# A feed-forward block with fp32 weights and one fp32 product per tile, in place of bf16 weights and two bf16 products

## The chip, the cores and the metric

The kernel runs on one Trainium2 chip, on all 8 NeuronCores at once. Each core computes half of the tokens of one of four sequences and needs nothing from the others. The metric is the device time of one execution in microseconds, which is that of the slowest core.

## The reference

```python
def reference(x, wq, wk, wv, wo, w_gate_up, w_proj):      # x: (4, 2048, 2048) fp32
    x = x + layernorm(attention(layernorm(x), wq, wk, wv, wo))   # 16 heads of 128, causal
    x = x + layernorm(ffn(layernorm(x), w_gate_up, w_proj))
    return x

def ffn(x, w_gate_up, w_proj):                # 16384 x 2048 and 2048 x 8192, fp32
    gu = einsum('bsd,hd->bsh', x, ternary_quant(w_gate_up))
    gate, up = split(gu, 2)
    h = silu(gate) * up                       # 8192 wide
    return einsum('bsh,dh->bsd', rms_norm(h), ternary_quant(w_proj))

def ternary_quant(w_fp32, g=64):              # all of it in bf16
    w = w_fp32.astype(bfloat16)
    scale = clip(mean(abs(groups of 64 of w)), 1e-8)
    w_hat = clip(round(w / scale), -1, 1) * scale
    return w + (w_hat - w)
```

## The kernel before

Everything on the chip is held transposed: features on the 128 partitions, tokens in the free dimension. A core has 1024 tokens of its own and the 2048 tokens of its sequence for keys and values. A small planner (`Prog.emit`) writes one list of instructions per engine, in program order, with semaphore waits; nothing is reordered afterwards. A DMA that an engine issues waits on that engine's queue, so a late wait on the sync queue (SP) holds back every later load.

The stages follow each other:

- **`_attn1`** loops over 4 token blocks of 512. For each it normalises the block and then makes 16 output tiles each of k, v and q. A tile is 16 fp32 matmuls (128x128 weights, 512 columns for k and v, 256 for q) whose weights come in one slab of 1 MB, loaded into one of two halves of `AR_W` (lines 378 and 421). The v tiles are transposed on TensorE, copied to `ptb` (line 471) and stored to `v_scr`, with waits on earlier stores.
- **`_quant_gen`** runs between the tiles of `_attn1`, one step for each of the 192 tiles. A step makes the ternary weights of a 128x2048 piece. GpSimd issues its load (fp32 in DRAM, bf16 in SBUF, line 293), does the last two operations (lines 278 and 282) into the bf16 tile `QLND`, and issues the store to `wgu_hat` or `wp_hat` (line 286). There are two `QLND` buffers; a step waits for the store of the step two before.
- **`_attn2`** is the attention itself, head by head. **`_attn3`** is the output projection: 2 token blocks, each of 16 slabs of 16 fp32 matmuls with 512 columns (line 664), slab loads two ahead, and then the layer norm and the residual.
- **`_ffn`** loops over 4 blocks `fb` of 256 tokens. A block loads x1 (line 709) and normalises it into `AR_D` (`_ln_block`, its last DVE operations at lines 368 and 371). DVE then splits the 16 pieces of the result into a bf16 high part `LN2H` (line 721) and a bf16 low part `LN2L` (line 723).

In the **gate-up loop** of `_ffn` there are 64 steps `c`. A step needs two weight slabs of 512 KB, one for gate (line 733) and one for up (line 738), in one of two pairs of buffers; the load of a pair waits for the matmuls that last used it. The pair for c=1 waits for all that was issued before it, c=0 included. A step is 64 matmuls of 256 columns: 16 pieces, gate and up (lines 748 and 755), high and low part. Then ACT computes silu (line 761), DVE multiplies (line 764) and splits the product into `HH` and `HL` (lines 768 and 771), ACT squares it (line 774), and TensorE adds the square into a sum (line 778). This last matmul stands ahead of the next step's matmuls in TensorE's order.

In the **projection loop** there are 16 output tiles of 64 pieces, in 4 slabs each. Every slab load (line 812) waits for all matmuls emitted so far:

```python
wsl = [("sP", P_.cnt["sP"] if (sw or dm or ss) else 0)]
```

So a slab's load starts when the matmuls of the slab before have ended. A slab is 32 matmuls of 256 columns (line 827). A last layer norm, the residual and the store to `out` close the block.

Of the kernel before, what the change touches and what calls it, by code (L numbers as in the profile page):

```python
# [106 lines left out]
def _alloc(nc):  # L107
# [13 lines left out]
    for nm, shape, dt_ in (("wgu_hat", [D, GU], BF16), ("wp_hat", [HF, D], BF16),  # L121
                           ("k_scr", [D, S], F32), ("v_scr", [S, D], F32),
                           ("q_scr", [D, TOK], F32), ("x1_scr", [D, TOK], F32)):
        if nm in _DBG_OUTS:
            DR[nm] = nc.dram_tensor(nm, shape, dt_, kind="ExternalOutput").ap()
        else:
            DR[nm] = nc.dram_tensor(nm, shape, dt_).ap()
# [37 lines left out]
    T["AR_WB"] = at("AR_WB", [128, 8192], BF16, 180224)  # L165

# [530 lines left out]
def _ffn(P_, T, DR):  # L697
# [3 lines left out]
    l2h = lambda k: T["LN2H"].ap()[:, k * 256:(k + 1) * 256]  # L701
    l2l = lambda k: T["LN2L"].ap()[:, k * 256:(k + 1) * 256]
    hh = lambda c: T["HH"].ap()[:, c * 256:(c + 1) * 256]
    hl = lambda c: T["HL"].ap()[:, c * 256:(c + 1) * 256]
    wb = lambda q: T["AR_WB"].ap()[:, q * 2048:(q + 1) * 2048]

    x1_ok = P_.snap("dC") + P_.snap("dQ")
    for fb in range(4):
# [9 lines left out]
        sp = None  # L718
        for k in range(KC):
            ws = [("sV", ln2_done), ("sP", P_.cnt["sP"])] if k == 0 else []  # L720
            P_.emit("dve", lambda e, k=k: e.tensor_copy(out=l2h(k), in_=lnD(k)),
                    waits=ws, inc="sV", tag=f"fsh{fb}.{k}")
            sp = P_.emit("dve", lambda e, k=k: e.tensor_tensor(  # L723
                out=l2l(k), in0=lnD(k), in1=l2h(k), op=ALU.subtract),
                inc="sV", tag=f"fsl{fb}.{k}")
        slabs = {}
        hsq_mm = None
        for c in range(64):
            r = c % 2
# [13 lines left out]
            mmu = None
            for k in range(KC):
                ws = [sl_g, sl_u, ("sV", sp)] if k == 0 else []
                for p, rhs_f in ((0, l2h), (1, l2l)):
                    P_.emit("pe", lambda e, gbank=gbank, r=r, k=k, rhs_f=rhs_f, p=p:
                            e.matmul(gbank, wb(2 * r)[:, k * 128:(k + 1) * 128],  # L748
                                     rhs_f(k), start=(k == 0 and p == 0),
                                     stop=(k == KC - 1 and p == 1)),  # L750
                            waits=ws if p == 0 else [], inc="sP",
                            tag=f"fg{fb}.{c}.{k}.{p}")
                    ws = []
                    mmu = P_.emit("pe", lambda e, ubank=ubank, r=r, k=k, rhs_f=rhs_f,
                                  p=p: e.matmul(  # L755
                                      ubank, wb(2 * r + 1)[:, k * 128:(k + 1) * 128],
                                      rhs_f(k), start=(k == 0 and p == 0),
                                      stop=(k == KC - 1 and p == 1)),
                                  inc="sP", tag=f"fu{fb}.{c}.{k}.{p}")
            slabs[r] = mmu  # L760
            sv = P_.emit("act", lambda e, gbank=gbank: e.activation(  # L761
                out=T["tmp"].ap()[:, 0:256], in_=gbank, func=AF.Silu),
                waits=[("sP", mmu)], inc="sA", tag=f"fsilu{fb}.{c}")
            ht = P_.emit("dve", lambda e, ubank=ubank: e.tensor_tensor(  # L764
                out=T["tmp"].ap()[:, 256:512], in0=T["tmp"].ap()[:, 0:256],
                in1=ubank, op=ALU.mult),
                waits=[("sA", sv)], inc="sV", tag=f"fht{fb}.{c}")
            P_.emit("dve", lambda e, c=c: e.tensor_copy(
                out=hh(c), in_=T["tmp"].ap()[:, 256:512]), inc="sV",
                tag=f"fhh{fb}.{c}")  # L770
            hv = P_.emit("dve", lambda e, c=c: e.tensor_tensor(
                out=hl(c), in0=T["tmp"].ap()[:, 256:512], in1=hh(c),
                op=ALU.subtract), inc="sV", tag=f"fhl{fb}.{c}")
            hq = P_.emit("act", lambda e: e.activation(
                out=T["LNXB"].ap()[:, 0:256], in_=T["tmp"].ap()[:, 256:512],
                func=AF.Square),
                waits=[("sV", ht)], inc="sA", tag=f"fhsq{fb}.{c}")
# [23 lines left out]
        for sw in range(2):  # L801
            for dm in range(8):
# [3 lines left out]
                for ss in range(4):  # L806
                    half = ss % 2
                    wsl = [("sP", P_.cnt["sP"] if (sw or dm or ss) else 0)]
                    if dc == 0 and ss == 0:
# [3 lines left out]
                                     out=wb(half).rearrange(  # L813
# [6 lines left out]
                    for kk in range(16):  # L820
# [4 lines left out]
                        for p, h_f in ((0, hh), (1, hl)):  # L825
                            mm = P_.emit("pe", lambda e, bank=bank, half=half,
                                         kk=kk, hk=hk, h_f=h_f, p=p: e.matmul(  # L827
                                             bank, wb(half)[:, kk * 128:
                                                            (kk + 1) * 128],
                                             h_f(hk), start=(hk == 0 and p == 0),  # L830
                                             stop=(hk == 63 and p == 1)),
                                         waits=ws if p == 0 else [], inc="sP",
                                         tag=f"fp{fb}.{dc}.{hk}.{p}")
                            ws = []
# [123 lines left out]
```

How the kernel before makes its waits and increments, by code:

```python
        def rnd(eng_obj, recs, own_sem=None):  # L71
            last_own = 0
            for waits, fn, inc, post, tag in recs:
                if own_sem is not None and last_own > 0 and fn is not None:
                    eng_obj.wait_ge(sems[own_sem], last_own)
                for (sem, v) in waits:
                    if v > 0:
                        eng_obj.wait_ge(sems[sem], v)
                if fn is not None:
                    ins = fn(eng_obj)
                    if inc is not None:
                        ins.then_inc(sems[inc], 16 if inc.startswith("d") else 1)
                if inc == own_sem and post is not None:
                    last_own = post
```

## Time and profile before

| | us |
|---|---|
| median of 2 runs | 16716.96 (16678.73 to 16755.19) |
| the profiled execution, its own time | 16731.51 |
| its span on the slowest core (core 1) | 16729.6 |
| spans of the 8 cores | 16537.4 to 16729.6 |
| attention, first to last instruction before the feed-forward block, core 1 | 0 to 10983 |
| feed-forward block, core 1 | 10983 to 16730 |

The spans are those of one execution under the profiler. A "record" below is one entry of the trace for one instruction. A matmul record's duration includes the drain of the array, so successive records overlap; the distance between their starts is what one costs in a stream. "PEclk" is the clock that the throttle granted to TensorE as a share of full speed. The mean over the whole run lies between 0.678 and 0.689 on the 8 cores.

### The profile page before, as it was taken

How to read it: one execution, taken by the hardware profiler on the slowest of the kernel's cores; microseconds unless marked ns; L12 is line 12 of the kernel's file. 1: busy time of each engine (PE TensorE's matmuls, PEld its weight loads, DVE VectorE, ACT ScalarE, POOL GpSimd, SP SyncE). 2: the span in 40 equal slices, each digit the busy share in tenths (PEclk: the TensorE clock that was granted, in tenths of full speed). 3: DMA queues.
4: the chain of work that ended last, by engine and by line, in shares of the span. 5: the costliest groups of instructions: out<-in, count | busy, mean ns of one | idle time of the engine just before them, and what ended most of it. 6: DMA issues, size and time to landing. Idle time of an engine off the chain costs nothing.

```text
span 16729.6 us, 137588 instructions; the slowest of 8 cores (16537.4 to 16729.6 us)
## 1 busy us (share of the span) xinstructions
PE 10050.8 (60%) x39456; PEld 5798.5 (35%) x39456; DVE 4080.1 (24%) x8274; ACT 1926.1 (12%) x2699; POOL 1768.1 (11%) x772
## 2 busy tenths in 40 slices
PE   6655866776676544444444546757548655754864
PEld 2222323223222322222222223336326434533643
DVE  3334434434443422222222221121011001001100
ACT  2122212222222200000000000000000000000000
POOL 2233323223332300000000000000000000000000
PEclk7666666666667655555555557879769768966976
DMA  3223323232332300000000001234224224422422
GB/s 83 68 75 83 85 68 89 80 80 77 86 82 72 93 7 13 7 13 7 13 7 13 7 13 30 71 92 102 52 54 115 66 46 96 92 52 63 113 59 48
DMA packets 2253436, 992.82 MB, mean 59 GB/s; under 512 B 1605317, under 2 KB 2178886, under 8 KB 2250566
## 3 DMA queue, kind: packets, MB, share of 16 engines
q1 hardware_dynamic: 2137542, 732.31, 17.3%
q0 software_dynamic: 55296, 201.35, 5.4%
q10 hardware_dynamic: 59904, 50.36, 0.9%
q8 instruction: 380, 6.23, 0.2%
q14 instruction: 314, 2.57, 0.1%
HBM read 925.17 MB, written 159.38 MB: 65 GB/s over the span
## 4 chain that ended last, share of the span: by engine, by line
PE 54%; DVE 15%; DMA 12%; issue 8%; ACT 5%; POOL 3%; DVEq 1%; ACTq 0%; SPq 0%; POOLq 0%
PE pbG L421 14%; PE pbH L623 7%; DMA AR_WB<-wp_hat 6%; PE pbG L748 6%; PE pbH L755 5%; PE pbG L610 3%; DMA v_scr<-ptb 3%; DVE ptb L617 3%; PE pbG L664 3%; PE pbE L531 3%; PE pbF L827 2%; PE pbE L827 2%; PE pbH L827 2%; PE pbG L827 2%; POOL QLND L282 2%
## 5 line engine op out<-in xcount | busy, mean ns | idle before, releaser
L421 PE MATMUL pbG<-AR_C,AR_W 128*128 128x512 f32 x4096 | 2369.5, 751 | 102.3 <-DVE AR_C L371 102.3
L623 PE MATMUL pbH<-ptb,AR_B 128*128 128x128 f32 x2944 | 1128.7, 487 | 1047.1 <-DVE ptb L617 1047.1
L421 PEld LDWEIGHTS pbG<-AR_C,AR_W 128*128 128x128 f32 x4096 | 970.8, 241 | 1437.2 <-issue 1437.2
L610 PE MATMUL pbG<-ident_t,AR_B 128*128 128x128 f32 x1472 | 656.2, 446 | 976.2 <-DVE AR_B L597 973.5
L748 PE MATMUL pbG<-LN2H,AR_WB 128*128 128x256 bf16 x4096 | 1127.5, 275 | 180.9 <-DVE LN2L L723 128.4
L623 PEld LDWEIGHTS pbH<-ptb,AR_B 128*128 128x128 f32 x2944 | 738.2, 312 | 1436.4 <-issue 1436.4
L278 POOL TENSOR_TENSOR QSG<-QT,QW 128x2048 bf16<-128x2048 bf16 x192 | 776.6, 4045 | 3871.0 <-DVE QT L273 3871.0
L755 PE MATMUL pbH<-LN2H,AR_WB 128*128 128x256 bf16 x4096 | 1128.3, 275 | 0.0
L748 PE MATMUL pbG<-LN2L,AR_WB 128*128 128x256 bf16 x4096 | 1128.0, 275 | 0.0
L755 PE MATMUL pbH<-LN2L,AR_WB 128*128 128x256 bf16 x4096 | 1127.8, 275 | 0.0
L617 DVE COPY ptb<-pbG 128x128 f32<-128x128 f32 x1472 | 428.8, 291 | 2209.4 <-PE pbG L610 2209.4
L230 DVE TENSOR_SCALAR QSCL<-pbE 2x512 bf16<-2x512 f32 x768 | 523.0, 681 | 1448.4 <-PE pbE L222 1301.2
L282 POOL TENSOR_TENSOR QLND<-QW,QSG 128x2048 bf16<-128x2048 bf16 x192 | 777.1, 4047 | 39.7 <-POOL QSG L278 39.4
L222 PE MATMUL pbE<-QABS,b_t 128*2 128x512 bf16 x768 | 265.7, 551 | 854.2 <-ACT QABS L208 713.4
L610 PEld LDWEIGHTS pbG<-ident_t,AR_B 128*128 128x128 f32 x1472 | 267.5, 182 | 1343.0 <-issue 1334.9
L421 PE MATMUL pbH<-AR_C,AR_W 128*128 128x256 f32 x2048 | 658.0, 499 | 0.0
L764 DVE TENSOR_TENSOR tmp<-tmp,pbH 128x256 f32<-128x256 f32 x256 | 107.8, 421 | 2071.1 <-ACT tmp L761 2071.1
L531 PE MATMUL pbE<-AR_B 128*128 128x512 f32 x480 | 443.1, 1074 | 261.7 <-DMA AR_B<-q_scr 203.6
L421 PEld LDWEIGHTS pbH<-AR_C,AR_W 128*128 128x128 f32 x2048 | 522.2, 259 | 134.5 <-issue 28.2
L263 DVE TENSOR_TENSOR QT<-QABS,QBB 128x512 bf16<-128x512 bf16 x768 | 535.2, 697 | 97.4 <-DVE QBB L257 37.7
L273 DVE TENSOR_TENSOR QT<-QT,QBB 128x512 bf16<-128x512 bf16 x768 | 531.5, 692 | 83.2 <-DVE QT L268 4.1
L827 PE MATMUL pbE<-HH,AR_WB 128*128 128x256 bf16 x1024 | 358.8, 367 | 284.9 <-DMA AR_WB<-wp_hat 284.9
(123 smaller groups left out, 11406.2 us busy)
## 6 DMA issues: line engine op xcount, KB each, us to landing
AR_WB<-wgu_hat SPq DMA_DIRECT2D x512, 512.0 KB, 6.3
AR_WB<-wp_hat SPq DMA_DIRECT2D x256, 512.0 KB, 4.1
QW<-wguT POOLq DMA_DIRECT2D x128, 512.0 KB, 8.6
AR_W<-wkT SPq DMA_DIRECT2D x64, 1024.0 KB, 9.2
wgu_hat<-QLND POOLq DMA_DIRECT2D x128, 512.0 KB, 5.9
AR_W<-wvT SPq DMA_DIRECT2D x64, 1024.0 KB, 5.7
AR_W<-wqT SPq DMA_DIRECT2D x64, 1024.0 KB, 6.0
QW<-wpT POOLq DMA_DIRECT2D x64, 512.0 KB, 7.9
```

The lines of the kernel that those rows point to most:

```text
L263: t_tok[(i, q)] = P_.emit("dve", lambda e, q=q: e.tensor_tensor(out=tt[:, q * 512:(q + 1) * 512], in0=absw[:, q * 512:(q + 1) * 512], in1= ...
L273: tsg_tok[(i, q)] = P_.emit("dve", lambda e, q=q: e.tensor_tensor(out=tt[:, q * 512:(q + 1) * 512], in0=tt[:, q * 512:(q + 1) * 512], in1= ...
L278: d_tok[i] = P_.emit("gp", lambda e: e.tensor_tensor(out=sg, in0=tt, in1=w, op=ALU.subtract), waits=[("sV", tsg_tok[(i, 3)])], inc="sG", t ...
L282: wf = P_.emit("gp", lambda e: e.tensor_tensor(out=laund, in0=w, in1=sg, op=ALU.add), waits=ws, inc="sG", tag=f"q_wf{i}")
L421: e.matmul(bank, T["AR_W"].ap()[:, half * 2048 + k * 128: half * 2048 + (k + 1) * 128], rhs, start=(k == 0), stop=(k == KC - 1)),
L531: mm = P_.emit("pe", lambda e, t_=t_, c_=c_, kb=kb, qt=qt: e.matmul(t_[:, c_:c_ + 512], qh[:, qt * 128:(qt + 1) * 128], kh[:, kb * 512:(kb ...
L610: tr = P_.emit("pe", lambda e, trb=trb, kc=kc: e.transpose(trb, prob[:, kc * 128:(kc + 1) * 128], T["ident"][:]), waits=ws, inc="sP", tag= ...
L617: te = P_.emit("dve", lambda e, trb=trb, pcol=pcol: e.tensor_copy(out=T["ptb"].ap()[:, pcol:pcol + 128], in_=trb), waits=tew, inc="sV", ta ...
L623: e.matmul(abank, vT[:, kc * 128:(kc + 1) * 128], T["ptb"].ap()[:, pcol:pcol + 128], start=(kc == 0), stop=(kc == W // 128 - 1)),
L748: e.matmul(gbank, wb(2 * r)[:, k * 128:(k + 1) * 128], rhs_f(k), start=(k == 0 and p == 0), stop=(k == KC - 1 and p == 1)),
L755: p=p: e.matmul(ubank, wb(2 * r + 1)[:, k * 128:(k + 1) * 128], rhs_f(k), start=(k == 0 and p == 0), stop=(k == KC - 1 and p == 1)),
L827: kk=kk, hk=hk, h_f=h_f, p=p: e.matmul(bank, wb(half)[:, kk * 128: (kk + 1) * 128], h_f(hk), start=(hk == 0 and p == 0), stop=(hk == 63 an ...
```

## The change

The quantised weights are kept in DRAM as fp32 in place of bf16, and the feed-forward block multiplies fp32 by fp32. What does that is this:

- `wgu_hat` and `wp_hat` are F32 tensors. GpSimd's store of a quantised piece now converts from bf16 to fp32 on its way and writes 1 MB, not 512 KB.
- The weight slabs in SBUF are four fp32 buffers of 1 MB (`FSLAB`) at another address, where `LN2H` and `LN2L` were.
- The two DVE operations per piece that made `LN2H` and `LN2L` are gone, and so are the two that made `HH` and `HL`. DVE writes the fp32 product directly into `hf32(c)`.
- Each pair of matmuls (high and low part against the same bf16 weights) becomes one fp32 matmul: 32 in place of 64 for a gate-up step, 16 in place of 32 for a projection slab.
- The first gate-up loads of a block wait also for DVE's and ACT's last emitted instruction, that is, for the end of the layer norm. Before, they waited for TensorE's alone.

```diff
-    for nm, shape, dt_ in (("wgu_hat", [D, GU], BF16), ("wp_hat", [HF, D], BF16),
+    for nm, shape, dt_ in (("wgu_hat", [D, GU], F32), ("wp_hat", [HF, D], F32),
...
+    T["FSLAB"] = at("FSLAB", [128, 8192], F32, 65536)
...
+    hf32 = lambda c: T["AR_A"].ap()[:, c * 256:(c + 1) * 256]
+    fsl = lambda q: T["FSLAB"].ap()[:, q * 2048:(q + 1) * 2048]
...
-        sp = None
-        for k in range(KC):
-            ws = [("sV", ln2_done), ("sP", P_.cnt["sP"])] if k == 0 else []
-            P_.emit("dve", lambda e, k=k: e.tensor_copy(out=l2h(k), in_=lnD(k)),
-                    waits=ws, inc="sV", tag=f"fsh{fb}.{k}")
-            sp = P_.emit("dve", lambda e, k=k: e.tensor_tensor(
-                out=l2l(k), in0=lnD(k), in1=l2h(k), op=ALU.subtract),
-                inc="sV", tag=f"fsl{fb}.{k}")
...
-            wsl = [("sP", slabs[r])] if r in slabs else                 [("sP", P_.cnt["sP"])] + list(x1_ok)
+            wsl = [("sP", slabs[r])] if r in slabs else                 [("sP", P_.cnt["sP"]), ("sV", P_.cnt["sV"]),
+                 ("sA", P_.cnt["sA"])] + list(x1_ok)
...
-                ws = [sl_g, sl_u, ("sV", sp)] if k == 0 else []
-                for p, rhs_f in ((0, l2h), (1, l2l)):
...
+                ws = [sl_g, sl_u, ("sV", ln2_done)] if k == 0 else []
+                P_.emit("pe", lambda e, gbank=gbank, r=r, k=k:
+                        e.matmul(gbank, fsl(2 * r)[:, k * 128:(k + 1) * 128],
+                                 lnD(k), start=(k == 0), stop=(k == KC - 1)),
+                        waits=ws, inc="sP", tag=f"fg{fb}.{c}.{k}")
+                mmu = P_.emit("pe", lambda e, ubank=ubank, r=r, k=k: e.matmul(
+                    ubank, fsl(2 * r + 1)[:, k * 128:(k + 1) * 128],
+                    lnD(k), start=(k == 0), stop=(k == KC - 1)),
+                    inc="sP", tag=f"fu{fb}.{c}.{k}")
...
-            P_.emit("dve", lambda e, c=c: e.tensor_copy(
-                out=hh(c), in_=T["tmp"].ap()[:, 256:512]), inc="sV",
-                tag=f"fhh{fb}.{c}")
-            hv = P_.emit("dve", lambda e, c=c: e.tensor_tensor(
-                out=hl(c), in0=T["tmp"].ap()[:, 256:512], in1=hh(c),
-                op=ALU.subtract), inc="sV", tag=f"fhl{fb}.{c}")
...
-                        for p, h_f in ((0, hh), (1, hl)):
...
+                        mm = P_.emit("pe", lambda e, bank=bank, half=half,
+                                     kk=kk, hk=hk: e.matmul(
+                                         bank, fsl(half)[:, kk * 128:
+                                                         (kk + 1) * 128],
+                                         hf32(hk), start=(hk == 0),
+                                         stop=(hk == 63)),
+                                     waits=ws, inc="sP",
+                                     tag=f"fp{fb}.{dc}.{hk}")
```

## Rows read from the trace of the kernel before

**Rows 1.** Spans and mean granted TensorE clock of two cores.

```profile
core 1: 16729.6 us, clock 0.686
core 2: 16673.3 us, clock 0.679
```

**Rows 2.** Windows, core 1: length, busy PE, PEld, DVE, ACT, POOL (records), PEclk, DMA share, GB/s.

```profile
11061.00:11647.00 586.00, 469.63 (x4091) 396.19 (x4092) 70.68 (x186) 49.66 (x124) 0.00 (x0) 0.99 0.49 114
11665.00:12340.00 675.00, 366.91 (x2052) 258.15 (x2052) 19.52 (x48) 7.46 (x18) 0.00 (x0) 0.71 0.22 49
```

**Rows 3.** SP's issues, core 1: gate slab loads of two steps, and the x1 loads.

```profile
11096.21 0.36 SPq L733 DMA_DIRECT2D AR_WB<-wgu_hat  x1
...
11105.36 0.36 SPq L733 DMA_DIRECT2D AR_WB<-wgu_hat  x1
...
L709 SPq DMA_DIRECT2D AR_D<-x_scr x4: 367/370/370, 10982.8 to 15289.7; - x4
```

**Rows 4.** Timeline of PE, core 1, gate-up (start us, us): two records, 15 apart.

```profile
11099.82 0.27 PE L748 MATMUL pbG<-LN2H,AR_WB 128*128 128x256 bf16 x1
...
11101.46 0.27 PE L755 MATMUL pbH<-LN2L,AR_WB 128*128 128x256 bf16 x1
```

**Rows 5.** Projection, core 1: 63 loads on SP; then PE's total wait for them.

```profile
11665.04 633.89 SPq L812 DMA_DIRECT2D AR_WB<-wp_hat  x63
...
  DMA AR_WB<-wp_hat: 1142.6, 256
```

**Rows 6.** fp32 matmuls, core 1: chain row of attn3, q burst, windows in that burst.

```profile
10648.61 221.91 PE pbG L664 x512
...
1124.67 9.45 PE L421 MATMUL pbH<-AR_C,AR_W 128*128 128x256 f32 x32
...
1124.70:1134.50 9.80, 9.41 (x33) 7.60 (x32) 7.90 (x15) 1.60 (x4) 0.00 (x0) 0.77 0.00 0
...
1130.00:1133.00 3.00, 3.00 (x16) 2.64 (x15) 2.51 (x5) 0.00 (x0) 0.00 (x0) 1.00 0.00 0
```

**Rows 7.** DMA issues: count, KB each, median us from issue to landing.

```profile
AR_WB<-wgu_hat SPq DMA_DIRECT2D x512, 512.0 KB, 6.3
AR_WB<-wp_hat SPq DMA_DIRECT2D x256, 512.0 KB, 4.1
AR_W<-wkT SPq DMA_DIRECT2D x64, 1024.0 KB, 9.2
...
AR_W<-woT SPq DMA_DIRECT2D x32, 1024.0 KB, 5.5
```

**Rows 8.** Block start, core 1: first and last of 32 split operations; PE's slab waits.

```profile
11032.80 0.29 DVE L721 CAST LN2H<-AR_D 128x256 bf16<-128x256 f32 x1 [0.24 <-DVE AR_D L371]
...
11047.44 0.42 DVE L723 TENSOR_TENSOR LN2L<-AR_D,LN2H 128x256 bf16<-128x256 f32 x1
...
PE pbG L748 <- DMA AR_WB<-wgu_hat: 31.9, 4, 8.8
```

**Rows 9.** Core 2: windows of attn3 and of gate-up 1 and 4; loads as rows 3.

```profile
9844.00:10100.00 256.00, 255.53 (x485) 108.46 (x486) 0.00 (x0) 8.96 (x15) 0.00 (x0) 0.81 0.21 61
10760.00:11300.00 540.00, 453.09 (x3254) 353.00 (x3255) 57.41 (x151) 40.00 (x100) 0.00 (x0) 0.80 0.42 98
...
15340.00:15900.00 560.00, 458.65 (x3766) 377.24 (x3765) 66.12 (x174) 46.40 (x116) 0.00 (x0) 0.93 0.47 109
...
11101.96 0.36 SPq L733 DMA_DIRECT2D AR_WB<-wgu_hat  x1
...
11144.41 0.36 SPq L733 DMA_DIRECT2D AR_WB<-wgu_hat  x1
...
L709 SPq DMA_DIRECT2D AR_D<-x_scr x4: 366/370/370, 10617.6 to 15213.1; - x4
```

**Rows 10.** Core 1: GpSimd's wait (us, times, longest); chain of v phase 1 by line.

```profile
POOL QSG L278 <- DVE QT L273: 3871.0, 192, 152.3
...
by line: PE pbG L421 50.6%; DMA v_scr<-ptb 23.0%; ACT QABS L208 5.0%; issue 4.7%; PE pbF L245 4.0%; PE pbE L222 3.4%; DVE ptb L471 2.0%; DVE QSCL L230 1.8%; PE pbH L460 1.5%; ACT stg L448 1.5%; PE pbE L245 1.1%; ACTq L478 0.5%; ACTq L78 0.3
```

More of the change, by code:

```diff
@@ L700, in _ffn @@
     lnY = lambda k: T["AR_D"].ap()[:, 4096 + k * 256: 4096 + (k + 1) * 256]
[L701 to L705, printed above, removed]
+    hf32 = lambda c: T["AR_A"].ap()[:, c * 256:(c + 1) * 256]
+    fsl = lambda q: T["FSLAB"].ap()[:, q * 2048:(q + 1) * 2048]
     x1_ok = P_.snap("dC") + P_.snap("dQ")
@@ L731, in _ffn @@
             ubank = (pbH[:, 0:256], pbH[:, 512:768])[r]
-            wsl = [("sP", slabs[r])] if r in slabs else                 [("sP", P_.cnt["sP"])] + list(x1_ok)
+            wsl = [("sP", slabs[r])] if r in slabs else                 [("sP", P_.cnt["sP"]), ("sV", P_.cnt["sV"]),
+                 ("sA", P_.cnt["sA"])] + list(x1_ok)
             sl_g = P_.emit("sync", lambda e, c=c, r=r: e.dma_start(
-                out=wb(2 * r).rearrange("p (kk t) -> p kk t", kk=16),
+                out=fsl(2 * r).rearrange("p (kk t) -> p kk t", kk=16),
                 in_=DR["wgu_hat"].rearrange("(kk p) m -> p kk m", p=128)[
@@ L738, in _ffn @@
             sl_u = P_.emit("sync", lambda e, c=c, r=r: e.dma_start(
-                out=wb(2 * r + 1).rearrange("p (kk t) -> p kk t", kk=16),
+                out=fsl(2 * r + 1).rearrange("p (kk t) -> p kk t", kk=16),
                 in_=DR["wgu_hat"].rearrange("(kk p) m -> p kk m", p=128)[
@@ L744, in _ffn @@
             for k in range(KC):
-                ws = [sl_g, sl_u, ("sV", sp)] if k == 0 else []
-                for p, rhs_f in ((0, l2h), (1, l2l)):
[L747 to L759, printed above, removed]
+                ws = [sl_g, sl_u, ("sV", ln2_done)] if k == 0 else []
[7 more added lines that the diff above has]
+                    inc="sP", tag=f"fu{fb}.{c}.{k}")
             slabs[r] = mmu
@@ L763, in _ffn @@
                 waits=[("sP", mmu)], inc="sA", tag=f"fsilu{fb}.{c}")
-            ht = P_.emit("dve", lambda e, ubank=ubank: e.tensor_tensor(
-                out=T["tmp"].ap()[:, 256:512], in0=T["tmp"].ap()[:, 0:256],
+            hprev = [("sP", hsq_mm)] if c >= 1 else []
+            ht = P_.emit("dve", lambda e, ubank=ubank, c=c: e.tensor_tensor(
+                out=hf32(c), in0=T["tmp"].ap()[:, 0:256],
                 in1=ubank, op=ALU.mult),
                 waits=[("sA", sv)], inc="sV", tag=f"fht{fb}.{c}")
-            P_.emit("dve", lambda e, c=c: e.tensor_copy(
-                out=hh(c), in_=T["tmp"].ap()[:, 256:512]), inc="sV",
-                tag=f"fhh{fb}.{c}")
-            hv = P_.emit("dve", lambda e, c=c: e.tensor_tensor(
-                out=hl(c), in0=T["tmp"].ap()[:, 256:512], in1=hh(c),
-                op=ALU.subtract), inc="sV", tag=f"fhl{fb}.{c}")
[L774 to L777, printed above, removed]
+            hq = P_.emit("act", lambda e, c=c: e.activation(
+                out=T["LNXB"].ap()[:, 0:256], in_=hf32(c), func=AF.Square),
+                waits=[("sV", ht)] + hprev, inc="sA", tag=f"fhsq{fb}.{c}")
             hsq_mm = P_.emit("pe", lambda e, c=c: e.matmul(
@@ L812, in _ffn @@
                                  e.dma_start(
-                                     out=wb(half).rearrange(
+                                     out=fsl(half).rearrange(
                                          "p (kk t) -> p kk t", kk=16),
@@ L824, in _ffn @@
                             ws.append(("sV", yv[7]))
-                        for p, h_f in ((0, hh), (1, hl)):
[L826 to L834, printed above, removed]
+                        mm = P_.emit("pe", lambda e, bank=bank, half=half,
[6 more added lines that the diff above has]
+                                     tag=f"fp{fb}.{dc}.{hk}")
                 yv[dm] = P_.emit("dve", lambda e, bank=bank, dc=dc: e.tensor_tensor(
```

## The prediction

> **What bounds the kernel now.** I read the spans and granted clocks first. The slowest core is core 1 with 16729.6 us, and core 2 is 56 us behind it [rows 1]; the execution itself took 16731.5 us, 14.5 us over the median of 16717, so the sum below is made against 16731 and holds for the median within 0.1%. Then the windows of the feed-forward block on core 1. Gate-up has 64 steps in 586 us with TensorE busy 80% of it at a granted clock of 0.99 [rows 2]. One step takes 11105.36 - 11096.21 = 9.15 us [rows 3]. Fifteen record starts lie 1.64 us apart, so a 256-column bf16 matmul costs 0.1093 us [rows 4], 64 of them 7.00 us, and the other 2.15 us are the tail silu, multiply, square, sum matmul, during which TensorE stands still. The slab loads aren't in it: they land 6.3 us after issue [rows 7] and are issued a whole step ahead. Gate-up is thus bound by TensorE's stream plus a fixed tail.
>
> The projection is bound by TensorE and the loads in turn. 63 loads take 633.89 us, so one slab takes (633.89 - 0.36) / 62 = 10.22 us; TensorE waits 1142.6 / 256 = 4.46 us for each, and a burst of 32 matmuls takes the rest, 5.7 us [rows 5]. At full clock it would take 3.5 us. The mean clock there is 0.71 [rows 2]: every burst starts at the lower level (1.2 GHz) after its wait and rises to 2.4 GHz some 4 us in. A block lasts (15289.7 - 10982.8) / 3 = 1435.6 us [rows 3], of which 586 + 654 are these two loops.
>
> **The fp32 matmul.** A token block of the output projection has 16 x 16 = 256 fp32 matmuls of 512 columns and shows 512 records in 221.91 us [rows 6]. So an fp32 matmul is two records. Taking off some 2 us for the slow start, a record costs 0.4295 us at full clock, and half of it, 0.2147 us, with 256 columns. The q tiles have just that shape: 32 records in 9.45 us with a clock of 0.77 [rows 6]. From 0.77, 46% of the window or 4.5 us were at half clock; 32 x 0.2147 + 4.5 / 2 = 9.1 us, and 9.45 less the last record's drain is the same. The weight loads (PEld, 2.64 us in a full-clock window of 3 us) stay below the matmuls and are hidden [rows 6]. The change replaces two bf16 matmuls (0.219 us) by two fp32 records (0.429 us): TensorE's time for this work doubles, less nothing.
>
> **Gate-up.** 64 bf16 matmuls become 64 fp32 records: 64 x (0.2147 - 0.1093) = 6.75 us more per step, 9.15 -> 15.9 us, times 256 steps: **+1728 us**. The tail stays: the two split operations removed from DVE there start after the multiply, and what waits for the multiply (ACT's square) does not wait for them; they are worth nothing. The loads double to 2 MB per 15.9 us, 132 GB/s against 114 now [rows 2]. A pair issued a step ahead has 15.9 us to land. I take it as hidden; a pair would have to take over two and a half times today's 6.3 us to show.
>
> **Projection.** The burst: 32 fp32 records. With 4.2 to 4.5 us at half clock, 32 x 0.2147 + 2.2 = 9.1 us against 5.7, +3.4. The wait: the slab grows from 512 KB to 1 MB and its load isn't covered by anything. The nearest row is the slab of wo, same size, rows and stride, on an otherwise quiet machine: 5.5 us to landing against 4.1 [rows 7], +1.4 us. The bounds are 0 (a landing set by the number of pieces, which stays) and +5.1 (the wk slabs, 9.2 us, beside the quantiser's traffic [rows 7]). I take 1.4, as nothing else loads then. Sum +4.8 us, 256 slabs: **+1230 us** (low 870, high 2180).
>
> **Block starts.** The 32 split operations last from 11032.80 to 11047.86, 15.1 us with nothing beside them [rows 8]. They go. In their place the first pair of slabs, whose load now waits for the end of the layer norm, is exposed: the pair for c=1 is exposed today at up to 8.8 us for 1 MB, a mean of 8.0 [rows 8]; for 2 MB I take 10 us. So -5 us for c=0 and +2 for c=1: **-3 us** per block, -12 in all (between -30 and +20).
>
> **The quantiser.** The store of 1 MB goes out on GpSimd's queue, where only the next load is queued behind it. GpSimd idles 3871 us over 192 steps, 20 us each [rows 10], and a buffer has two steps until it is needed, so the store itself is hidden; without that cover it would be 192 times some 3 us. But it shares the DMA engines with the small v stores, which are 23% of the chain in the v phase [rows 10], some 500 us over the four. The trace has no store of that kind; the bound above is the 1.4 us that 512 KB more cost a slab [rows 7], on both store waits of 64 tiles, 180 us; below, nothing. I take **+80 us**.
>
> Sum on core 1: 1728 + 1230 - 12 + 80 = +3026, **19757 us**, if its clock stays as it is.
>
> **The clock.** Core 1 is not the core to look at. On core 2 the granted clock stands at 0.81 through the output projection, where 485 records take 256 us: 0.528 us each, which is 0.4295 / 0.81. It stands at 0.80 through gate-up and is back at 0.93 only in block 4 [rows 9]. Core 2 starts the feed-forward block 365 us before core 1, loses most of this through the lower clock and ends 56 us ahead [rows 1, 3, 9]. Its gate-up step takes (11144.41 - 11101.96) / 4 = 10.61 us, 0.132 us per matmul. After the change an fp32 record costs it 0.528 / 2 = 0.264: 64 x (0.264 - 0.132) = 8.4 us per step, 540 per block. In the projection the burst at full speed is some 22 records, 0.05 us longer each: 4.8 + 1.1 - 0.2 = 5.7 us per slab, 365 per block. So a block under this clock costs +902, one without (1728 + 1230 - 12) / 4 = +737. With core 2 held in three blocks of four as today: 16673 + 3 x 902 + 737 + 80 = 20196. **I forecast 20200 us**, set by core 2 or one like it.
>
> The Trainium skill (TensorE: Matmul & The Clock Gate, Part 1, the peak-current limiter) says that dense matmuls on three cores of a die take that die to 13/16 of the clock for as long as the load lasts. The 0.81 of rows 9 agrees in size; core 1's 0.99 in gate-up, while all cores work [rows 2], doesn't agree. By the page no core would see full clock, which is the third rival.
>
> **Rivals.**
> - *Core 2 is not released.* The longer, denser stream keeps 0.81 in block 4 too: + (902 - 737) and the 76 us by which that block was shorter than the mean of the first three (1532): 20440.
> - *The clock holds no one back in the feed-forward block.* Then core 1 sets the end: 19757. Against it: fp32 is the denser stream, 86% of a step instead of 77%.
> - *The limit takes core 1 in the feed-forward block as well.* Its four blocks would then cost 4 x (1532 + 902) from 10983 + 80: 20800.
> - *The loads show.* Projection slabs land as those of wk do: +3.7 x 256 = 950, 21150 with core 2. A quiet wo-like machine speaks against it.
> - *Not slower.* An fp32 matmul would have to be one record of bf16 cost, as if weights holding bf16 values took a short way. The 512 and 32 records speak against it. It would be 12288 records of 0.109 fewer, -1343, and + 360 for loads - 12 + 80: 15816. It decides where the mean fp32 record falls under 0.105 us, half of what is measured.
>
> **Chances.** Forecast 0.38; core 2 not released 0.20; no hold 0.15; core 1 held too 0.15; loads show 0.07; not slower 0.02; others 0.03. About 2% is what a measurement can tell from no change; all cases but one lie far above 17050, so slower 0.98, within 2% 0.01, faster 0.01. The range takes in the first four cases and leaves room for the projection's low bound: 19650 to 20850.
>
> **What would show it.** Right: fp32 records of 0.21 to 0.22 us spacing at clock 1.0, steps of 15.9 us and of 19.0 on a held core; projection waits of 5.9 us and bursts of 9.1; splits gone and 10 us of slab wait in their place; a v phase longer by 1 to 2 us per tile. Wrong: waits for slabs between gate-up steps, a landing far from 5.5, a burst that starts at full clock, or another pattern of 0.81 over the cores.

## The result, and the profile after

| | before | after |
|---|---|---|
| median, us | 16784.61 (10 runs, 16645.83 to 17259.89) | 20381.9 (11 runs, 20118.74 to 20885.64) |
| ratio of after to before | | 1.2114, 95% interval 1.2028 to 1.22 |
| profiled span of the slowest core, us | 16729.6 (core 1) | 20333.6 (core 0) |

The change made the kernel 21% slower. The forecast was 20200 us (19650 to 20850), slower with a chance of 0.98. The runs of before behind the ratio are more than the two known at the time of the forecast; their median is 68 us higher. Some executions of either kernel are some per cent longer, because the cores of one die are granted less clock in them; the medians and ranges include these, the ratios leave them out.

First the page of the slowest core after the change: the costliest matmul groups (count | busy us, mean ns of one | idle before, releaser) and the weight loads (count, KB each, us to landing).

```profile
L738 PE MATMUL pbG<-AR_D,FSLAB 128*128 128x256 f32 x8192 | 2791.9, 426 | 177.0 <-DMA FSLAB<-wgu_hat 159.4
L741 PE MATMUL pbH<-AR_D,FSLAB 128*128 128x256 f32 x8192 | 2766.9, 423 | 0.0
```

```profile
FSLAB<-wgu_hat SPq DMA_DIRECT2D x512, 1024.0 KB, 10.0
FSLAB<-wp_hat SPq DMA_DIRECT2D x256, 1024.0 KB, 5.5
```

The number of records is that of before: 16384 in gate-up, two for each fp32 matmul where there were two bf16 matmuls. The wp slab of 1 MB lands in 5.5 us, which is what the wo slab of the same size took [rows 7].

The gate-up loop and the clock, in windows (length, busy PE, PEld, DVE, ACT, POOL, PEclk, DMA share, GB/s). The first two rows are gate-up of blocks 1 and 3 on core 0, the next two the projection of blocks 2 and 3 there, the last two gate-up of blocks 1 and 3 on core 2; they answer to [rows 2, 9].

```profile
11000.00:12100.00 1100.00, 1003.67 (x3560) 816.16 (x3560) 22.75 (x54) 43.16 (x108) 0.00 (x0) 0.77 0.39 105
16000.00:17000.00 1000.00, 880.39 (x3735) 737.99 (x3734) 26.59 (x60) 47.26 (x116) 0.00 (x0) 0.94 0.45 119
...
14700.00:15600.00 900.00, 571.29 (x1787) 455.08 (x1785) 5.95 (x14) 0.00 (x0) 0.00 (x0) 0.70 0.22 65
17300.00:17800.00 500.00, 312.99 (x1052) 252.91 (x1053) 3.40 (x8) 0.00 (x0) 0.00 (x0) 0.78 0.23 67
...
10800.00:11700.00 900.00, 806.12 (x3434) 676.99 (x3434) 21.91 (x52) 41.56 (x104) 0.00 (x0) 0.94 0.43 124
...
15600.00:16500.00 900.00, 821.04 (x2915) 667.77 (x2916) 18.53 (x44) 35.52 (x89) 0.00 (x0) 0.77 0.42 105
```

There are two levels in gate-up. One is 0.77 to 0.79, a core held at 0.81 with short stretches at half clock. The other is 0.94, where the kernel before had 0.99 [rows 2]. Core 0 is held in blocks 1 and 2 and free in 3 and 4, core 2 the other way round. Each core is thus held in two blocks of four, and the eight cores end within 158 us of one another.

Now the part that was not foreseen. SP's gate loads on core 0 in block 3, one per step (start us, us), and TensorE over the start of one of those steps:

```profile
16213.68 0.36 SPq L724 DMA_DIRECT2D FSLAB<-wgu_hat  x1
...
16229.79 0.36 SPq L724 DMA_DIRECT2D FSLAB<-wgu_hat  x1
...
16247.59 0.36 SPq L724 DMA_DIRECT2D FSLAB<-wgu_hat  x1
```

```profile
16231.37 0.27 PE L757 MATMUL pbE<-LNXB,ones_t 128*1 128x256 bf16 x1 [1.71 <-ACT LNXB L754]
16231.72 0.67 PE L738 MATMUL pbG<-AR_D,FSLAB 128*128 128x256 f32 x2
16232.23 0.74 PE L741 MATMUL pbH<-AR_D,FSLAB 128*128 128x256 f32 x2
16232.76 1.06 PE L738 MATMUL pbG<-AR_D,FSLAB 128*128 128x256 f32 x2
16233.62 1.06 PE L741 MATMUL pbH<-AR_D,FSLAB 128*128 128x256 f32 x2
...
16236.07 0.59 PE L738 MATMUL pbG<-AR_D,FSLAB 128*128 128x256 f32 x2
16236.51 0.59 PE L741 MATMUL pbH<-AR_D,FSLAB 128*128 128x256 f32 x2
```

Steps take 16.11 or 17.80 us. Before the sum matmul of each of these steps TensorE stands still for 1.71 us; below, this standstill is the gap. In the kernel before it was 1.66 us:

```profile
11088.59 0.27 PE L778 MATMUL pbE<-LNXB,ones_t 128*1 128x256 bf16 x1 [1.66 <-ACT LNXB L774]
```

In a step of 17.80 us, pairs of fp32 records start 0.43 us apart at full clock, but soon after the gap they start 0.85 us apart for about 3.5 us, at the lower of the two levels (1.2 GHz). That costs some 1.7 us. A core is called free here where its clock is not held at 0.81. On a free core the mean step is 17.05 us, because the clock falls in 56% of the steps; on held cores it is 19.5 to 20.0 us.

The projection in the chain of waits on core 0, block 3 (start us, us): load, burst, load, burst.

```profile
17264.17 5.54 DMA FSLAB<-wp_hat
17269.84 9.02 PE pbE L805 x32
17278.98 5.49 DMA FSLAB<-wp_hat
17284.60 10.16 PE pbE L805 x32
```

The total wait of TensorE for these slabs, which answers to the 1142.6 us of [rows 5], is

```profile
  DMA FSLAB<-wp_hat: 1495.9, 256
```

that is 5.84 us each against 4.46. A slab takes 15.3 to 16.2 us against 10.2.

### The profile page after: what moved, and what is told of

It is laid out like the page before. It is cut to its first block, busy times and chain, and to the rows that moved or that the text cites. A ratio compares the mean times of both kernels' runs of the same rounds, so it can differ in the third digit from the quotient of the medians.

```text
span 20333.6 us, 136568 instructions; the slowest of 8 cores (20176.0 to 20333.6 us)
## 1 busy us (share of the span) xinstructions
PE 13332.2 (66%) x39456; PEld 8635.6 (42%) x39456; DVE 3851.1 (19%) x7634; ACT 1925.1 (9%) x2699; POOL 1768.4 (9%) x772
## 4 chain that ended last, share of the span: by engine, by line
PE 61%; DMA 12%; DVE 11%; issue 7%; ACT 5%; POOL 3%; DVEq 1%; ACTq 0%; SPq 0%; POOLq 0%
PE pbG L422 11%; PE pbG L738 10%; PE pbH L741 10%; DMA FSLAB<-wp_hat 7%; PE pbH L624 6%; PE pbH L805 3%; PE pbF L805 3%; PE pbG L805 3%; PE pbE L805 3%; PE pbG L611 3%; PE pbG L665 3%; DVE ptb L618 2%; PE pbE L532 2%; DMA v_scr<-ptb 2%; POOL QLND L283 1%
## 5 line engine op out<-in xcount | busy, mean ns | idle before, releaser
L738 PE MATMUL pbG<-AR_D,FSLAB 128*128 128x256 f32 x8192 | 2791.9, 426 | 177.0 <-DMA FSLAB<-wgu_hat 159.4
L741 PE MATMUL pbH<-AR_D,FSLAB 128*128 128x256 f32 x8192 | 2766.9, 423 | 0.0
L738 PEld LDWEIGHTS pbG<-AR_D,FSLAB 128*128 128x128 f32 x8192 | 1742.5, 215 | 516.2 <-issue 230.2
L741 PEld LDWEIGHTS pbH<-AR_D,FSLAB 128*128 128x128 f32 x8192 | 1765.4, 216 | 303.5
L805 PE MATMUL pbH<-AR_A,FSLAB 128*128 128x256 f32 x2048 | 629.9, 482 | 373.6 <-DMA FSLAB<-wp_hat 373.6
L805 PE MATMUL pbG<-AR_A,FSLAB 128*128 128x256 f32 x2048 | 626.4, 480 | 377.6 <-DMA FSLAB<-wp_hat 377.6
L805 PE MATMUL pbF<-AR_A,FSLAB 128*128 128x256 f32 x2048 | 627.7, 481 | 371.5 <-DMA FSLAB<-wp_hat 371.5
L805 PE MATMUL pbE<-AR_A,FSLAB 128*128 128x256 f32 x2048 | 618.0, 475 | 373.2 <-DMA FSLAB<-wp_hat 373.2
L805 PEld LDWEIGHTS pbH<-AR_A,FSLAB 128*128 128x128 f32 x2048 | 505.8, 251 | 497.9 <-issue 398.9
L805 PEld LDWEIGHTS pbG<-AR_A,FSLAB 128*128 128x128 f32 x2048 | 503.1, 249 | 502.1 <-issue 403.9
```

The source lines that it names most:

```text
L738: e.matmul(gbank, fsl(2 * r)[:, k * 128:(k + 1) * 128], lnD(k), start=(k == 0), stop=(k == KC - 1)),
L741: mmu = P_.emit("pe", lambda e, ubank=ubank, r=r, k=k: e.matmul(ubank, fsl(2 * r + 1)[:, k * 128:(k + 1) * 128], lnD(k), start=(k == 0), s ...
L805: kk=kk, hk=hk: e.matmul(bank, fsl(half)[:, kk * 128: (kk + 1) * 128], hf32(hk), start=(hk == 0), stop=(hk == 63)),
```

## The experiments

The theory: each step and each slab costs more for the reasons of the sum, and gate-up has an extra loss, the fall of the clock at the 1.7 us gap. Rivals: the extra loss comes from the projection half; it comes from the longer step and not from fp32; or fp32 drops the clock with or without a gap. One more was not thought of beforehand, and the traces speak to it: the change altered the gap itself, which is 0.05 us longer than before. Each run is compared with runs of the kernel before on the same chip; these had medians of 16640 us for `e1` to `e4`, 16643 us for `e5`, `e7`, `e8` and `e9`, and 16617 us (one run) for `e6` and `e12`.

### One half at a time

`e1` has fp32 in gate-up alone, `e2` in the projection alone.

```diff
# e1, from the changed kernel (with the projection loop of before)
-    for nm, shape, dt_ in (("wgu_hat", [D, GU], F32), ("wp_hat", [HF, D], F32),
+    for nm, shape, dt_ in (("wgu_hat", [D, GU], F32), ("wp_hat", [HF, D], BF16),
...
# e2, from the kernel before (with the projection loop of the change)
-    for nm, shape, dt_ in (("wgu_hat", [D, GU], BF16), ("wp_hat", [HF, D], BF16),
+    for nm, shape, dt_ in (("wgu_hat", [D, GU], BF16), ("wp_hat", [HF, D], F32),
...
```

> Only the gate-up half of the change: w_gate_up in fp32 and fp32 matmuls there, the projection as before (bf16 weights, high and low part). The recorded sum had gate-up at +6.75 us a step, 256 steps, and -12 us at block starts: about +1720, some 18500 us. The trace of the changed kernel shows steps of 17.05 us where the clock is not held and 19.5 to 20.05 where it is, against 9.2 and 10.7 before. If that is the gate-up loop's own doing, this kernel gains 7.85 x 256 = 2010 us with no core held, and some 2300 with two blocks of four held: 18800 to 19150 us. If the longer steps come from what the projection half does to the clock, it stays at 18500 and the step at 15.9 us.

> Only the projection half of the change: w_proj in fp32 and fp32 matmuls there, gate-up as before. The recorded sum had +4.8 us a slab, 256 slabs: +1230, some 18000 us, as +3.4 for the burst and +1.4 for the wait. The changed kernel's trace has a wait of 5.84 us (+1.38) and blocks of 966 to 1020 us for 64 slabs against 643 to 646: +5.0 to +5.8 us a slab, 1290 to 1490 us. Expected 18000 to 18250. e1 and e2 should add up to the whole change within some 150 us; if they do not, the two halves act on each other through the clock.

Measured: `e1` 18763.18 us (4 runs, 18575.73 to 18855.13), +2123 on its before (ratio 1.1238, interval 1.1106 to 1.1369); `e2` 18336.39 us (4 runs, 18155.44 to 18513.24), +1697. Gate-up windows of blocks 1 and 4 in `e1` on core 0, and one of its sum matmuls:

```profile
11200.00:12200.00 1000.00, 897.04 (x3813) 752.29 (x3812) 67.25 (x177) 47.20 (x118) 0.00 (x0) 0.94 0.43 122
...
17000.00:18000.00 1000.00, 897.16 (x3798) 752.07 (x3797) 67.25 (x177) 47.20 (x118) 0.00 (x0) 0.94 0.51 123
```

```profile
11311.79 0.27 PE L766 MATMUL pbE<-LNXB,ones_t 128*1 128x256 bf16 x1 [1.66 <-ACT LNXB L762]
```

With bf16 in the projection the gate-up clock is 0.94 all the same, and the steps take 17.05 us in all four blocks of this core. So the loss is the gate-up loop's own. The gap is 1.66 us here, as in the kernel before, and the clock falls after 59% of the gaps of this core; before, on free cores, it fell after 3 to 5%. `e1` ends just below what was expected, because in its profiled execution the slowest core is not held in this part at all.

`e2` ends above its range. Its projection takes 966 to 1012 us a block, about as expected, but its bf16 gate-up steps take 10.2 to 10.8 us in the mean of a block, against 9.2 to 9.3 on core 1 before. This is not the hold at 0.81. Core 0 is free in block 3, and its clock is 0.90 there, with bf16 records alone; the timeline is that of a gap in block 1, where it is free too:

```profile
14600.00:15150.00 550.00, 451.94 (x3486) 363.38 (x3484) 22.73 (x54) 43.16 (x108) 0.00 (x0) 0.90 0.44 104
```

```profile
11016.36 0.27 PE L775 MATMUL pbE<-LNXB,ones_t 128*1 128x256 bf16 x1 [1.71 <-ACT LNXB L772]
...
11017.47 0.27 PE L758 MATMUL pbH<-LN2L,AR_WB 128*128 128x256 bf16 x1
11017.58 0.27 PE L751 MATMUL pbG<-LN2H,AR_WB 128*128 128x256 bf16 x1
...
11018.07 0.42 PE L758 MATMUL pbH<-LN2L,AR_WB 128*128 128x256 bf16 x1
11018.28 0.42 PE L751 MATMUL pbG<-LN2H,AR_WB 128*128 128x256 bf16 x1
```

From 11017.86 to 11021.06 the bf16 records start 0.21 us apart in place of 0.11: the lower level. The clock falls after 56 to 61% of the gaps in this bf16 stream, and steps take 9.22 or 10.87 us. TensorE's own work in this loop is that of the kernel before. What differs around it is the gap, 1.71 us against 1.66, and that DVE no longer makes its two split operations beside it; `e2` does not separate these two. The 0.05 us come from the tail: the product goes to `AR_A` and the square reads it there, and the square starts 0.57 us after the multiply has started, where it was 0.51. All kernels with the product in `AR_A` and the gap left in (`e2`, `e4`, `e7`, the change) show 1.71, those with it in `tmp` (before, `e1`, `e3`, `e12`) 1.66.

The two halves add up to 3820 us, the whole change to 3597. The falls are one likely reason: they come in `e1` and in `e2`, some 240 us a core in each, and only once in the whole. Single executions scatter by about as much, so the difference proves nothing by itself.

### Is it the fp32 stream or the longer step?

```diff
# e3: the kernel before, each step's sums made twice
-            for k in range(KC):
+            for k in list(range(KC)) * 2:
# e4: the changed kernel, half of the pieces
-            for k in range(KC):
+            for k in range(KC // 2):
...
-                    lnD(k), start=(k == 0), stop=(k == KC - 1))
+                    lnD(k), start=(k == 0), stop=(k == KC // 2 - 1))
```

> The kernel before, with every gate-up step's 64 bf16 matmuls issued twice (the second set starts the sums anew, so the result stays): a bf16 stream of 14.0 us and then the same tail of 2.15 us with 1.7 us of standstill. In the changed kernel the clock falls to the lower level after about two of three such tails, before it almost never did. Theory kind: the fall hangs on fp32 records. Then this kernel keeps a granted clock of 0.98 to 1.0 in gate-up and a step is 16.15 us. Theory length: the fall hangs on the longer step around the same tail. Then the clock is 0.94, steps are 16.1 and 17.8 us mixed, mean 17.0.

> The changed kernel with only the first 8 of the 16 pieces multiplied in gate-up (half of the sum over features is left out): 32 fp32 records, a stream of 6.9 us and the same tail, so a step as long as the one before the change. Theory kind: the clock still falls after many tails; each fall costs some 1.7 to 2 us, the mean clock in gate-up is 0.85 to 0.92 and the mean step 9.9 to 10.7 us. Theory length: the clock stays at 0.98 or more as before and the step is 9.0 us. The loads of 2 MB a step now have 9 us to land, against 10.0 to landing in the changed kernel, so waits for slabs may show between steps; the clock at the start of a step that did not wait for a slab tells the theories apart.

Measured: `e3` 18592.22 us (2 runs, 18472.74 and 18711.69), `e4` 19088.82 us (1 run; it leaves out half of each sum). `e3` on core 0 in block 2: a window; two gate loads on SP; and the sum matmul after the second on TensorE.

```profile
12700.00:13600.00 900.00, 802.72 (x7163) 697.14 (x7160) 63.11 (x167) 44.47 (x112) 0.00 (x0) 1.00 0.28 65
```

```profile
13001.64 0.36 SPq L733 DMA_DIRECT2D AR_WB<-wgu_hat  x1
...
13017.77 0.36 SPq L733 DMA_DIRECT2D AR_WB<-wgu_hat  x1
```

```profile
13019.29 0.27 PE L778 MATMUL pbE<-LNXB,ones_t 128*1 128x256 bf16 x1 [1.66 <-ACT LNXB L774]
```

A step of 16.13 us with the gap of 1.66 us, and the clock stays at 1.00. On free cores it falls after 2 to 3% of these gaps. `e1` is its counterpart, with the same gap and nearly the same step (16.05 us without a fall), and there it falls after 59%. So on a free core, at this gap, the length of the step does not bring the fall and the change to fp32 does. On a held core the length counts too. In block 1 on core 2 of `e3` the bf16 clock falls below the 0.81 after 66% of gaps of 1.66 us; in the kernel before, with its short steps, it did so after 19% on the same core. The window:

```profile
10900.00:11800.00 900.00, 820.51 (x5877) 651.09 (x5876) 52.48 (x138) 36.84 (x92) 0.00 (x0) 0.78 0.24 55
```

`e4` in block 3 on core 2 is the other side, an fp32 step as short as that of bf16, here one in which no slab was waited for:

```profile
15021.55 0.27 PE L757 MATMUL pbE<-LNXB,ones_t 128*1 128x256 bf16 x1 [1.71 <-ACT LNXB L754]
15021.90 0.67 PE L738 MATMUL pbG<-AR_D,FSLAB 128*128 128x256 f32 x2
...
15023.15 1.06 PE L738 MATMUL pbG<-AR_D,FSLAB 128*128 128x256 f32 x2
15024.01 1.06 PE L741 MATMUL pbH<-AR_D,FSLAB 128*128 128x256 f32 x2
...
15026.25 0.59 PE L738 MATMUL pbG<-AR_D,FSLAB 128*128 128x256 f32 x2
```

The clock falls, in a step of 10.9 us. Its gap is 1.71 us, and `e2` shows the same with bf16 at such a gap, so `e4` shows only that a fall needs no long step; by itself it says nothing of fp32. The kind of matmul, what happens at the gap and, on a held core, the length all move the share of gaps with a fall. Which property of the stream lies behind them is open. The price of `e4` is not that of falls alone: its loads land 12.5 us after issue on core 2 (up to 14.4 on others), later than a step is long, so many steps wait for a slab, 4.4 us in the step before this one. Its mean steps are 12.4 to 14.3 us, well above the 9.9 to 10.7 expected. It also marks where the hidden gate-up loads stop being hidden.

### Taking the gap away

```diff
             slabs[r] = mmu
+            if pend is not None:
+                hsq_mm = pend()
...
-            hsq_mm = P_.emit("pe", lambda e, c=c: e.matmul(
-                pbE[0:1, 0:256], T["ones1"][:], T["LNXB"].ap()[:, 0:256],
+            pend = lambda c=c, r=r, hq=hq, fb=fb: P_.emit("pe", lambda e: e.matmul(
+                pbE[0:1, 0:256], T["ones1"][:],
+                T["LNXB"].ap()[:, r * 512:r * 512 + 256],
...
+        hsq_mm = pend()
```

> The changed kernel with the sum matmul of step c issued behind the matmuls of step c+1 (squares in two buffers), so TensorE does not stand still between gate-up steps. Theory gap: the clock falls in the changed kernel because an fp32 stream is interrupted for 1.7 us. Then without the gap the granted clock in gate-up is 1.0 where a core is not held, a step is 64 x 0.2147 + 0.1 = 13.85 us against 17.05, and the whole is some 800 us shorter, 19550 us. Theory kind alone: fp32 records drop the clock whatever stands between them. Then the clock stays at 0.94 and a step is 14.7 us, 19800 us. If the denser stream makes the 0.81 hold catch both groups of cores at once, steps are 17.0 us in more than two of four blocks and the time stays above 19900.

Measured: 19332.04 us (4 runs, 19267.78 to 19396.23), some 200 us less than expected. `pend()` issues the sum matmul of the step before. Core 0: a window in gate-up of block 1, and the gate loads of two steps on SP.

```profile
11200.00:11900.00 700.00, 700.00 (x3203) 598.90 (x3202) 20.63 (x49) 39.16 (x98) 0.00 (x0) 1.00 0.53 149
```

```profile
11507.59 0.36 SPq L725 DMA_DIRECT2D FSLAB<-wgu_hat  x1
...
11521.81 0.36 SPq L725 DMA_DIRECT2D FSLAB<-wgu_hat  x1
```

TensorE is busy all the time and the clock is 1.00 from fp32 records alone. A step is 14.22 us: 13.74 for the stream and 0.48 for the sum matmul and its two changes of kind, 0.37 more than expected. Of the 17.05 us of a free step, 2.8 hung on the gap, some 1.9 of them as standstill (16.11 against 14.22) and some 0.95 as the fall. The rival by which fp32 lowers the clock without a gap has fallen. The one by which a denser stream is held in more blocks is not borne out either: this core, the slowest, is free in all four (steps of 14.2 to 14.3 us), and that is where the time went below the expected 19550.

### Taking the projection's waits away

`e7` is the changed kernel with each slab load waiting only for its own buffer, of four.

```diff
-                    wsl = [("sP", P_.cnt["sP"] if (sw or dm or ss) else 0)]
-                    if dc == 0 and ss == 0:
-                        wsl = [("sV", r5), ("sP", P_.cnt["sP"])]
+                    wsl = [("sP", pfree[half])] if half in pfree else gu_done
```

> The changed kernel with the projection's slab loads issued up to four slabs ahead, each waiting only for the last matmul on its own buffer. Tests the two terms of the projection sum, wait 5.84 us and slow start 2.2 us of a slab of 15.1 to 15.9. Both should go: a slab is then 32 x 0.2147 = 6.9 us at a clock of 1.0, a block's projection 440 to 470 us in place of 966 to 1020, and the kernel 18200 to 18400 us. Rival: the loads set the pace, 1 MB in 6.9 us being 152 GB/s a core; e4 shows 2 MB landing in 12.5 us, 6.3 us per MB, so the margin is small, and a slab may cost 7 to 8 us with waits for slabs left.

Measured: 18006.36 us, one execution, below the 18200 to 18400 expected. The 64 loads of block 1 on core 0, and a window in them:

```profile
11956.73 425.67 SPq L791 DMA_DIRECT2D FSLAB<-wp_hat  x64
```

```profile
12000.00:12350.00 350.00, 349.32 (x1619) 307.22 (x1618) 5.09 (x12) 0.00 (x0) 0.00 (x0) 1.00 0.52 151
```

The last load goes out four slabs before the end, so a slab takes 425.3 / 60 = 7.09 us. That is the stream of 32 x 0.2147 = 6.87 us and little else, at 151 GB/s. It confirms that of the 15.4 us of a free slab 8.3 were wait and slow start.

### What is left, and a version that beats both

`e8` is the kernel before, bf16, with both edits; `e9` the changed kernel with both; `e6` and `e12` are bf16 with one each.

> The kernel before (bf16, high and low part) with both: the sum matmul one step late and the projection loads four slabs ahead. Gate-up step 64 x 0.1093 + 0.1 = 7.1 to 7.3 us in place of 9.2, projection slab 3.5 to 3.8 us in place of 10.2: 2.0 x 256 + 6.5 x 256 = 2180 us less, 14500 us. Rival: 512 KB per 3.5 us is 150 GB/s in 256-byte rows; if the loads bind, as 1 MB of such rows landed 6.3 us after issue, slabs cost 4 to 4.5 us and the kernel 14650 to 14750.

> The changed kernel with both. If the waits are gone, what is left between this and e8 is the price of the fp32 matmul alone: records of 0.2147 against 0.1093 us, 24576 of them a core: 0.1054 x 24576 = 2590 us, with the two gains 20382 - 800 - 2100 = 17450 us against e8's 14500. If the hold at 0.81 takes more of the time on the denser stream, 17700 to 18300.

> The kernel before with the sum matmul one step late, nothing else. Splits the gain of e8 in its two parts. In the bf16 kernel the clock did not fall at the gap, so only the standstill itself can go: a free step 64 x 0.1093 + 0.4 = 7.4 us in place of 9.2 and some 450 us in all, 16200 us. e8 however showed steps of 8.0 to 8.8 us with waits for gate-up slabs at 92 of 256 steps. If the denser stream is what brings the hold (0.81: 8.6 us a step), the loop gains only 0.5 to 1 us a step here too, 16400 to 16500 us.

> The kernel before with the projection loads up to four slabs ahead, nothing else. The other part of e8. In e8 the projection of a block took 217 us where the clock was free and 252 to 260 where it was held, against 643 before. Expected the same here: 4 x (643 - 230) = 1650 us less, 15000 us, so that e6 and e12 together give e8's 1800.

| | us | against its before |
|---|---|---|
| `e8`, bf16 with both | 14817.12 (5 runs, to 15123.43) | 16643.41 (7 runs, from 16598.07) |
| `e9`, fp32 with both | 17365.69 (5 runs) | 16643.41 |
| `e6`, bf16, gap gone | 16304.83 (2 runs) | 16616.57 (1 run) |
| `e12`, bf16, loads ahead | 14938.12 (1 run) | 16616.57 (1 run) |

`e9` less `e8` is 2549 us by the medians, and the price of the fp32 records by the sum, 24576 x 0.1054, is 2590. That they agree this well is partly chance, since the cores of the two kernels were not held alike. The cores that were never held in the feed-forward block (0, 1, 6 and 7 of `e8`; 0 to 3, 6 and 7 of `e9`) took 3757 to 3794 us from the first x1 load to the end in `e8` and 6227 to 6250 in `e9`, some 2460 more. So the record price is confirmed within 5%. It comes out a little low, as the gate-up steps of `e8` wait for slabs and are longer than their stream and sum matmul, while those of `e9` wait at block starts almost alone.

`e8` beats both kernels, by 11% and 27%. Its slowest run is 1475 us under the fastest of before. Its projection takes 217 us a block where it was 643, with a window in it:

```profile
11562.56 216.95 SPq L817 DMA_DIRECT2D AR_WB<-wp_hat  x64
```

```profile
11590.00:11760.00 170.00, 169.32 (x1552) 151.54 (x1551) 5.10 (x12) 0.00 (x0) 0.00 (x0) 1.00 0.66 150
```

It ends above the expected 14500, as its gate-up steps take 8.0 to 8.8 us and not 7.2. Part of that is the hold, part the loads, which show as waits now (us, times, longest):

```profile
PE pbG L749 <- DMA AR_WB<-wgu_hat: 148.5, 92, 11.0
```

`e12` alone gains 1678 us and `e6` alone 312, between its two expectations; together they would be 1990, and `e8` has 1826. On the cores that were never held in the feed-forward block the gains do add up: this part takes 5747 to 5751 us before, 4048 to 4063 in `e12` and 5454 to 5458 in `e6`, that is 1690 and 290 less, and 3757 to 3794 in `e8`. `e6` waits for gate-up slabs as `e8` does (129 us in all on core 0, against 32 before on core 1 [rows 8]). So in bf16 the gain from closing the gap is partly lost to these loads. It is not simply the rate of 256-byte rows: the projection of `e8` takes the same rows at 150 GB/s, four slabs ahead and with the rows less far apart in DRAM, and waits 18 us for them in all. Whether the lead of one step or the distance of the rows limits gate-up, no run separates.

## Why the prediction was right, point by point

- **fp32 record 0.2147 us at full clock, two per matmul.** Right: 16384 + 8192 records, pairs 0.43 us apart, and 0.528 / 2 on held cores. The free cores of `e9` and `e8` give the whole term within 5%.
- **Gate-up step 15.9 us free, 19.0 held.** The term was sized too small: 17.05 free, 19.5 to 20.0 held. The step of it that failed is "the tail stays", in two ways. Without a fall of the clock a step is 16.11 us, 0.2 over the forecast. Of that, 0.05 is the longer gap: taking the split operations away was held to be worth nothing, but with them the product moved to `AR_A`. The larger part is that the clock now falls at the gap in 56% of the steps, 0.94 us in the mean. Together it is 1.15 us over 256 steps, 294 us on a core that is never held. I had read the granted clock of 0.99 around the gap in the bf16 loop as something that would stay [rows 2]. It depends on the stream (`e1` against `e3`) and on small changes at the gap (`e2` against the kernel before), and it goes when the gap goes (`e5`).
- **Projection: wait +1.4, burst +3.4.** The wait was right, 5.84 against 4.46, and wo's slab was the row to take. The burst was 9.5 us (a free slab of 15.4 less 5.84), against 9.1: about 4.8 us of it are at the lower level, where the forecast took 4.2 to 4.5. On the same core it was 4.9 before, so the slow start itself did not change. A free slab takes 15.3 to 15.4 us against 15.0 forecast, a held one up to 16.2 against 15.9.
- **Block starts: -5 and +2.** The first fp32 matmul of block 1 stands 59.9 us behind the x1 load (10906.49 - 10846.58) against 65.2 (core 0 after, core 1 before): -5.3. The wait for the second pair grew from 8.0 to about 12.6 us, not to 10. Both are small.
- **The quantiser: +80.** Wrong in size: hardly anything is to be seen. The mask load that ends this part, on two cores whose clock is hardly held in it (0.74 before, core 4; 0.75 in `e9`, core 0), before and with the fp32 store:

```profile
L504 SPq DMA_DIRECT2D AR_B<-qmask x1: 341/341/341, 5362.3 to 5362.3; - x1
```

```profile
L505 SPq DMA_DIRECT2D AR_B<-qmask x1: 340/340/340, 5346.3 to 5346.3; - x1
```

  Over all cores of the kept traces that are held for at most 2% of this part, it lies between 5320 and 5362 us with both stores in bf16 and between 5336 and 5366 with `wgu_hat` in fp32, so the store is worth some 15 us at most. On held cores this part takes up to 5824 and 5820 us. The clock decides it and the store hardly does. The large v store waits of core 1 [rows 10] were those of a held core: 406.6 us in all on core 1 and 393.9 on core 0, which was held like it, 196.7 on core 4, which was not.
- **Which core sets the end.** The mechanism was right, the pattern not. A core like core 2, held in three blocks of four, was forecast. In the profiled execution all are held in two, cores 0, 1, 6 and 7 in blocks 1 and 2 and cores 2 to 5 in blocks 3 and 4. The errors, +294 from the falls and one held block fewer (165 us) with no 80 from the quantiser, nearly cancel: 20200 forecast, 20382 measured. So the middle of the forecast was hit partly by luck; by its own terms it was some 300 us short in gate-up.
- **Rivals.** "The loads show" is out in the changed kernel (waits for gate slabs only at block starts, 159.4 us in all) and real in `e4`. "Not slower" is out. That core 1 or its like is held through the whole feed-forward block did not happen in the profiled execution. In the sum of "core 2 is not released" the 76 us should read 72 (block 4 took 1460 us against 1532), which changes nothing.

The limiter rule of the Trainium skill named in the prediction (TensorE: Matmul & The Clock Gate, Part 1) would have every core of a loaded die held for as long as the load lasts. The windows above show one group at 0.77 and the other at 0.94 under the same load, and the two change places between blocks 2 and 3. `e5` shows core 0 at 1.00 through all four blocks with a denser stream on every core. The level agrees with the rule, its "as long as" doesn't. Nor is a die held as a whole: in all kept traces the hold goes by pairs of cores, as the last section shows.

## What to carry to other kernels

An fp32 matmul of 256 columns costs 0.429 us here and two bf16 matmuls cost 0.219. So where the weights hold bf16 values anyway, splitting the moving operand into two bf16 parts costs half as much as fp32, even before the weight bytes, and is worth its few DVE operations. Before a precision is changed, take the waits out of the loops around it: here a load that waited for all earlier matmuls, and a small matmul in line behind a chain of ACT and DVE, were worth 1826 us. And do not carry a granted clock from one stream to another: another kind of matmul around a gap changed it here, and so did a gap 0.05 us longer with two DVE operations fewer beside it. Read it in rows of the same kind with the same gaps, or leave room for it.

## What the runs showed that I had not expected

- Whether a standstill of 1.7 us brings TensorE to its lower level hangs on small things. On free cores it did after 3 to 5% of gaps of 1.66 us in the bf16 kernel before (steps of 9.15 us) and 2 to 3% in `e3` (16.13 us), but after 59% of the same gaps between fp32 streams (`e1`), and after 56 to 61% of gaps of 1.71 us between bf16 streams, with two DVE operations fewer beside them (`e2`). Without the gap the fp32 stream keeps 1.00 (`e5`). Why, the runs don't say; a series of gap lengths in one kernel would be the next thing to run.
- The level of 0.81 goes by pairs of cores, 0 and 1, 2 and 3, 4 and 5, 6 and 7: within a pair the held stretches nearly coincide in every kept trace. Which pairs go together changes. After the change they were 0, 1, 6, 7 against 2 to 5. In `e3`, from 16700 to 17500 us, cores 0, 1, 4 and 5 stand at 0.78 to 0.79 and 2, 3, 6 and 7 at 1.00; in the kernel before, from 14000 to 14300 us, only cores 2 and 3 are held (0.79 and 0.80). What makes it move is open. No run here was made to find out, since all cores run one program.
- It moves single executions of one kernel by some per cent, and the parts of a change then don't add up better than that: 3820 against 3597 us, of which the falls counted twice are a part as far as can be seen.
